# Post-LN layer with a test-time-trained attention scan: three turns moved to TensorE, and the order of VectorE, SyncE and ScalarE work changed

## The reference, cut to what matters

```
k = rotary(x @ Wk.T); v = x @ Wv.T                # per head, 32 features
W = eye(32)                                       # one state per batch and head
for each mini-batch of 16 tokens:
    z = kc @ W
    W = W - kc.T @ ((z - vc) * 2/(16*32))
x1 = layernorm(x + layernorm(z_all, gamma, beta) @ Wo.T)
g = (x1 @ gate_w.T) * gate_s; u = (x1 @ up_w.T) * up_s    # 1408 features, float32
out = layernorm(x1 + (silu(g) * u) @ down_w.T * down_s)
```

## Time and profile before

| | |
|---|---|
| median of three runs | 2067.89 us |
| the profiled execution's own time | 2065.14 us |
| its span | 2062.9 us |
| TensorE busy, matmuls | 1871.4 us (91%) |
| VectorE busy | 1175.4 us (57%) |
| ScalarE busy | 544.1 us (26%) |
| GpSimd busy | 642.3 us (31%) |
| DMA, queue of SyncE | 47.3% of 16 engines' span |

### The profile page before, as it was taken

How to read it: one execution, slowest core, us unless ns; L and a number is a source line. 1 busy time by engine, 2 the same in 40 slices (tenths; PEclk the granted TensorE clock), 3 DMA queues, 4 the chain that set the end, 5 groups by cost and what they waited for, 6 DMA issues and landing times.

```text
span 2062.9 us, 60543 instructions
## 1 busy us (share of the span) xinstructions
PE 1871.4 (91%) x25752; PEld 1488.1 (72%) x25752; DVE 1175.4 (57%) x2618; ACT 544.1 (26%) x1230; POOL 642.3 (31%) x776
## 2 busy tenths in 40 slices
PE   5556999999999999999999999999999999999897
PEld 4335777777777777777777777777777777777676
DVE  4354655665565566556556655655665565566543
ACT  2012222322222222222222222222322222232222
POOL 1012333333333333333332333333333333333233
PEclk9667999999999999999999999999999999999999
DMA  8583455545445554444455444455545445554310
GB/s 253 182 281 97 124 150 147 156 127 148 142 126 150 147 159 132 141 138 137 141 147 158 134 138 139 125 151 148 157 127 145 142 129 148 145 150 122 109 57 22
DMA packets 306800, 292.48 MB, mean 142 GB/s; under 512 B 42977, under 2 KB 255073, under 8 KB 306529
## 3 DMA queue, kind: packets, MB, share of 16 engines
q1 hardware_dynamic: 305248, 288.07, 47.3%
q10 hardware_dynamic: 1280, 0.53, 0.1%
HBM read 155.27 MB, written 141.82 MB: 144 GB/s over the span
## 4 chain that ended last, share of the span: by engine, by line
PE 63%; DMA 15%; DVE 11%; SPq 4%; issue 3%; ACT 3%; ACTq 0%; POOL 0%; DVEq 0%; POOLq 0%
PE gu_acc L755 26%; PE work L736 21%; PE down_acc L767 9%; DMA landed<-zT_scr 8%; DMA zT_scr<-turned 4%; PE scan_acc L725 3%; PE scan_acc L708 3%; SPq L336 2%; DVE turned L896 2%; DVE state L964 2%; DVE x_tok L891 2%; ACT hid L586 2%; DVE hid L969 2%; DMA z_scr<-v_rows 1%; DVE k_sin L946 1%
## 5 line engine op out<-in xcount | busy, mean ns | idle before, releaser
L520 POOL TENSOR_TENSOR hid_lo<-hid,hid_hi 128x256 fp32r<-128x256 f32 x352 | 262.0, 744 | 795.9 <-ACT hid_hi L596 795.8
L755 PE MATMUL gu_acc<-x_hi,gw 128*128 128x256 f32 x1372 | 377.6, 308 | 7.2 <-DVE hid L969 2.0
L586 ACT ACTIVATE hid<-gu_acc,gate_scale 128x256 f32<-128x256 f32 x343 | 162.6, 474 | 769.2 <-PE gu_acc L755 767.8
L755 PE MATMUL gu_acc<-x_hi,uw 128*128 128x256 f32 x1372 | 344.5, 283 | 0.0
L755 PE MATMUL gu_acc<-x_lo,uw 128*128 128x256 f32 x1372 | 343.1, 281 | 0.0
L755 PE MATMUL gu_acc<-x_lo,gw 128*128 128x256 f32 x1372 | 342.6, 281 | 0.0
L964 DVE SCALAR_TENSOR_TENSOR state<-scan_acc,half_step,state 128x256 f32<-128x256 f32 x512 | 223.1, 477 | 199.3 <-PE scan_acc L725 195.5
L969 DVE SCALAR_TENSOR_TENSOR hid<-gu_acc,up_scale,hid 128x256 f32<-128x256 f32 x343 | 165.5, 483 | 290.3 <-ACT hid L586 290.3
L755 PEld LDWEIGHTS gu_acc<-x_hi,gw 128*128 128x128 f32 x1372 | 257.5, 188 | 43.3 <-DVE hid L969 17.0
L767 PE MATMUL down_acc<-dw,hid_hi 128*128 128x512 f32 x704 | 282.3, 401 | 2.2 <-POOL hid_lo L520 2.1
L767 PE MATMUL down_acc<-dw,hid_lo 128*128 128x512 f32 x704 | 278.8, 396 | 0.0
(11 more groups left out here) (88 smaller groups left out, 2133.9 us busy)
## 6 DMA issues: line engine op xcount, KB each, us to landing
x_fm<-xT SPq DMA_DIRECT2D x64, 256.0 KB, 3.4
k_scr<-k_tok SPq DMA_DIRECT2D x32, 512.0 KB, 6.2
kT_scr<-turned SPq DMA_DIRECT2D x128, 128.0 KB, 2.9
kT<-kT_scr SPq DMA_DIRECT2D x32, 512.0 KB, 3.4
k_rows<-k_scr SPq DMA_DIRECT2D x512, 32.0 KB, 2.0
z_scr<-v_rows SPq DMA_DIRECT2D x32, 512.0 KB, 3.1
z_tok<-z_scr SPq DMA_DIRECT2D x512, 32.0 KB, 1.8
x_tok<-x SPq DMA_DIRECT2D x32, 512.0 KB, 3.9
```

Of the source, the lines that this page charges most:

```text
L520: pool.tensor_tensor(hid_lo[m % RING][:], hid[m % 2][:], hid_hi[m % RING][:].bitcast(F32), ALU.subtract).then_inc(hid_lo_ready, 1)
L586: act.activation(hid[m % 2][:], gu_bank(n, m)[:, 0:TOK], ACT.Silu, scale=gate_scale[:, m:m + 1]).then_inc(silu_done, 1)
L755: mm = pe.matmul(gu_bank(n, m)[:, k * TOK:(k + 1) * TOK], lhsT=w[:, c, m * P:(m + 1) * P].bitcast(dt), rhs=part[:, c].bitcast(dt), start=( ...
```

## The change

On TensorE, k of tiles 0, 1 and 2 (tick 0 slot 3, ticks 1 and 2 slot 6), zn of tile 0 (tick 2 slot 4) and x1 of tile 0 (tick 2 slot 10) are turned by transposes into PSUM. ScalarE copies k from PSUM to kT (`copy_kT`). VectorE's turns and the DRAM trips of these five are gone. On VectorE, both halves of `turn_zn` stand together ahead of `scale_hid` in slot 2; `normalize(2)` stands behind the statistics of zn in slot 0; `rotate(t+1, 0)` stands at the end of slot 12. On SyncE, the load of turned zn follows its store directly, the load of x comes behind it, and `out` is stored behind v of batch 0. FFN copies and loads go to ScalarE's queue: 10 copies (gate in 2, up in 4, down in 4) and 11 loads, one per scan slot or so. v rows of tile 1 go to that queue too. The buffer `half_step` is allocated later. The diff, cut to its core:

```
 SyncE, tick(t):
                 if within(sc) and sc >= 1:
                     load_k_half1(sc)
+                if within(sc) and sc >= ROW_TILES:
+                    load_v_half1(sc)
+                if within(t):
+                    store_v(t, 0)
                 if within(y):
                     sp.wait_ge(y_ready, 2 * y + 2)
                     sp.dma_start(out[...], y_tok[:]).then_inc(out_stored, 16)
-                if within(sc) and sc >= 1:
-                    load_v_half1(sc)
-                if t == 2:
-                    load_ffn(0, 0)
-                    load_ffn(0, 1)
-                if within(t):
-                    store_v(t, 0)
-                if within(o) and o != LAST:
+                if within(o) and z_by_dma(o):
                     store_znT(o)
+                    load_znT(o)
                 if within(o):
                     load_x(o)
-                if within(o) and o != LAST:
-                    load_znT(o)
...
-                if within(t) and t >= 1:
+                if within(t) and k_by_dma(t):
                     store_kT(t)
...
-                if within(t + 2):
+                if within(t + 2) and t != 1:
                     load_x_fm(t + 2)
...
+                if t == 1:
+                    load_x_fm(t + 2)

 ScalarE:
+            def load_v_rows(n, half):
+                act.wait_ge(v_stored, 32 * n + 32)
+                if n >= 1:
+                    act.wait_ge(state_added, 4 * NS * (n - 1) + 2 * NS * (half + 1))
+                    act.wait_ge(z_stored, 48 * (n - 1) + (16, 48)[half])
+                for g in range(NG):
...
+            def copy_kT(n, b):
+                act.wait_ge(k_turned, 2 * n + b + 1)
+                if n >= 1:
+                    act.wait_ge(k_cols_ready, 4 * n)
+                act.activation(kT[...], k_turn_bank(n, b)..., ACT.Copy).then_inc(kT_in, 8)
...
+                        copy_ffn(0, 0, 2)
+                    if within(t) and not k_by_dma(t) and s == 6:
+                        copy_kT(t, 0)
+                        copy_kT(t, 1)
+                    if t == 0 and s == 12:
+                        copy_ffn(0, 2, NC)
+                    if t == 1 and s in (0, 2, 4, 6):
+                        copy_ffn(1, s // 2, s // 2 + 1)
+                    if t == 1 and s in (8, 10, 12, 14):
+                        copy_ffn(2, 3 * (s // 2 - 4), min(3 * (s // 2 - 3), NM))
+                    if t == 2 and s in (0, 1, 2, 3):
+                        load_ffn(0, s, s + 1)
+                    if t == 2 and s in (4, 5, 6, 7):
+                        load_ffn(1, s - 4, s - 3)
+                    if t == 2 and s in (8, 9, 10):
+                        load_ffn(2, 4 * (s - 8), min(4 * (s - 7), NM))
+                    if t == 1 and s == 10:
+                        load_v_rows(1, 0)
+                    if t == 2 and s == 2:
+                        load_v_rows(1, 1)

 TensorE:
+            def turn_k(n):
+                if n == 0:
+                    pe.wait_ge(small_in, 16 * SMALL)
+                elif n == 1:
+                    pe.wait_ge(v_ready, 2)
+                else:
+                    pe.wait_ge(zn_low, 2)
+                for b in range(BATCH):
+                    pe.wait_ge(k_ready, 2 * n + b + 1)
+                    turn(k_turn_bank(n, b), k_tok, b, k_turned)
...
+                    if t == 0 and s == 3 or t in (1, 2) and s == 6:
+                        turn_k(t)
+                    if o == 0 and s == 4 or o == LAST and s == 5:
+                        turn_zn(o)
+                    if within(o) and not z_by_dma(o) and s == 10:
+                        turn_x1(o)

 VectorE, tick(t):
-                    if within(yn) and s == 0:
-                        normalize(2, yn, 0, y_tok, y_tok, y_ready)
-                        normalize(2, yn, 1, y_tok, y_tok, y_ready)
-                    if within(o) and o != LAST and s == 2:
+                    if within(o) and z_by_dma(o) and s == 2:
                         turn_zn(o, 0)
+                        turn_zn(o, 1)
...
-                    if within(t + 1) and s == 13:
-                        rotate(t + 1, 0)
...
                         moments_of(0, o)
+                    if within(yn) and s == 0:
+                        normalize(2, yn, 0, y_tok, y_tok, y_ready)
+                        normalize(2, yn, 1, y_tok, y_tok, y_ready)
...
-                    if within(o) and o != LAST and s == 2:
-                        turn_zn(o, 1)
...
+                    if within(t + 1) and s == 12:
+                        rotate(t + 1, 0)
                     for piece in WEIGHED.get((t, s), ()):
```

More of the change, by code:

```diff
@@ L229, in v_bank, with k_by_dma, kT_before, z_by_dma @@
             return (gu_acc, down_acc[1])[b] if n == 0 else work
-        LAST = NT - 1
+        def k_by_dma(n):
+            return n >= EARLY_TICKS
+        def kT_before(n):
+            return max(0, n - EARLY_TICKS)
+        def z_by_dma(n):
+            return n not in (0, LAST)
+        def zT_before(n):
+            return max(0, min(n, LAST) - 1)
+        def k_turn_bank(n, b):
+            return scan_acc[:, b, :] if n == 0 else (gu_acc, down_acc[1])[b][:]
+        def z_turn_bank(n, b):
+            return scan_acc[:, b, :] if n == LAST else (gu_acc, down_acc[1])[b][:]
         def by_token(buf, b):
@@ L238, in gu_bank, with turned_z @@
             return scan_acc[:, 2, :] if m % 2 and (n == LAST or n == LAST - 1 and m >= 3) else gu_acc[:]
[L240 to L248, removed]
+        def turned_z(n, b):
+            if z_by_dma(n):
+                return by_token(landed, b)
+            return z_turn_bank(n, b).rearrange("p (c a t) -> p c a t", c=NC, t=HEAD)
         def token_blocks(fm_buf, b):
@@ L399, in _ @@
             sp.wait_ge(zeroed, ZEROED)
[L401 to L412, removed]
             def tick(t):
@@ L606, in high_zn @@
             def high_zn(n, b):
-                if n == LAST:
+                if not z_by_dma(n):
                     act.wait_ge(zn_turned, 2 * n + b + 1)
                 elif b == 0:
-                    act.wait_ge(znT_in, 16 * (n + 1))
+                    act.wait_ge(znT_in, 16 * zT_before(n + 1))
                 if within(n + 2):
@@ L625, in high_x1 @@
             def high_x1(n, b):
-                if n == LAST:
+                if not z_by_dma(n):
                     act.wait_ge(x1_turned, 2 * n + b + 1)
                 elif b == 0:
-                    act.wait_ge(x1T_in, 16 * (n + 1))
+                    act.wait_ge(x1T_in, 16 * zT_before(n + 1))
                 if n >= 1:
                     act.wait_ge(gu_done, NM * n)
-                act.activation(token_blocks(x1_hi, b), turned_x1(n, b), ACT.Copy).then_inc(x1_hi_ready, 1)
-            def load_first_v():
-                act.wait_ge(v_stored, 32)
-                for half in range(2):
-                    for g in range(NG):
-                        b, hg = g // NC, g % NC
-                        act.dma_start(v_rows[g * MB:(g + 1) * MB, half * NS // 2:(half + 1) * NS // 2, g % 2, :],
-                                      v_scr[b, half * P // 2:(half + 1) * P // 2, hg * P:(hg + 1) * P]
-                                      .rearrange("(i t) c -> t i c", t=MB)).then_inc(rows_in[half], 16)
+                act.activation(token_blocks(x1_hi, b), turned_z(n, b), ACT.Copy).then_inc(x1_hi_ready, 1)
@@ new lines, in load_v_rows @@
+            def load_v_rows(n, half):
[4 more added lines that the diff above has]
+                for g in range(NG):
+                    b, hg = g // NC, g % NC
+                    act.dma_start(v_rows[g * MB:(g + 1) * MB, half * NS // 2:(half + 1) * NS // 2, g % 2, :],
+                                  v_scr[b, half * P // 2:(half + 1) * P // 2, hg * P:(hg + 1) * P]
+                                  .rearrange("(i t) c -> t i c", t=MB)).then_inc(rows_in[half], 16)
@@ L644, in _, with load_ffn @@
+            def load_ffn(i, c0, c1):
+                dst, src = ((gw, gw_scr), (uw, uw_scr), (dw, dw_scr))[i]
+                act.wait_ge(ffn_copied[i], 16 * COPIES[i])
+                act.dma_start(dst[:, c0:c1].bitcast(F32), src[c0 * P:c1 * P].rearrange("(c p) n -> p c n", p=P)
+                             ).then_inc(ffn_in[i], 16)
             act.wait_ge(wk_in, 16 * NC)
@@ L900, in turn_zn @@
                 dve.wait_ge(zn_ready, 2 * n + b + 1)
-                if b == 0 and n >= 1:
-                    dve.wait_ge(x1T_stored, 64 * n)
+                if b == 0 and n >= 2:
+                    dve.wait_ge(x1T_stored, 64 * zT_before(n))
                 turn(z_tok, b, zn_turned)
```

121 lines of the change are left out of this document (55 added, 66 removed).

## The result

The changed kernel takes 1959.34 us, the median of 4 runs (1953.75 to 1960.84). The kernel before takes 2068.91 us (4 runs, 2067.1 to 2076.71). The ratio is 0.9459, with a 95% interval of 0.9427 to 0.949. The profiled execution took 1957.84 us, its span 1956.0.

What follows compares the result with a forecast made beforehand. TensorE was taken as the bound in usual ticks, a chain of waits at the start. From 2065.14 us: -37 rotation, -31 zn, +14 normalize, -22 start gives 1989.1, 1992 with the median's 2.75; predicted 1991, range 1965 to 2028.

Steps and rivals of the forecast that it cites:

- item 3: Start: tile 0's z stores no longer queue behind a weight copy or v rows, so z's statistics come 10.5 us earlier.
- C: Rival: the moved normalize costs nothing and the zn residue is 0, giving 1971 us; chance 0.09.
- rotation: Slot 12: rotating ahead of the state update removes project_v's 1.33 us wait for the rotary product; 37 us in all.
- (a): Slot 2: the second zn turn, ahead of scale_hid, makes both turns end 0.9 us earlier.
- (b): SyncE's queue: turned zn, loaded ahead of x, lands up to 1.7 us sooner.
- 0.5 us for out: SyncE's queue: delay of the zn trip from out being stored just ahead of the store of zn.
- residue of 0.2 us a tick: project_o(0): zn wait expected to remain because single waits reach 3.0 us; 6 us in all.
- (1): Start, tick 0: turning tile 0's k on TensorE and copying it on ScalarE delays the row loads; cost 1.7 us.
- (2): Start, tick 1: turn_k adds 2.1 us behind scan_z, offset by the error step and earlier rotation; together 0.
- (4): Start: TensorE's turns of tile 0's zn replace project_o's 10.46 us wait for the DRAM trip; gain 4.2 us.
- (5): Start: the 6.65 us wait for tile 0's turned x1 and VectorE's two x1 turns go; gain 8 us.
- (6): Start: from VectorE's last weigh piece to TensorE's next work nothing changes; 0.

Runs made afterwards that it cites:

- a2: The kernel before with only rotate(t+1, 0) moved to the end of slot 12: 2032.68 us, ratio 0.9807.
- a4: The kernel after with the load of x issued ahead of the load of turned zn again: 1975.39 us, ratio 0.9533.
- b2: a3 with the second zn turn back behind scale_hid in slot 2: 1957.41 us, ratio 0.9446.
- b1: a3 with out stored ahead of the v rows of the scan's second half, as before: 1946.64 us, ratio 0.9392.
- d3: The kernel before with both zn turns ahead of scale_hid and turned zn loaded ahead of x: 2022.4 us, ratio 0.9762.
- b3: a3 with all four gate loads issued in slot 2 of tick 2 instead of slots 0 to 3: 1950.22 us, ratio 0.9405.
- c2: The kernel before with only the FFN weight copies and loads moved to ScalarE's queue, in pieces: 2067.64 us, ratio 0.9982.
- c4: The kernel after with only tick 2's rotation back in slot 13, behind the state update: 1963.51 us in one execution.
- c3: The kernel after with tile 0's zn and x1 turned by VectorE over DRAM again: 1967.94 us, ratio 0.9497.
- d2: The kernel after with the FFN weights back on SyncE's queue in their old pieces and places: 1964.78 us, ratio 0.9476.
- d1: The kernel before with all edits outside the start (rotation, zn turns, loads, out, normalize, half_step): 1981.33 us, ratio 0.9561.
- b4: The kernel after with 32 unused bytes per partition added where half_step stood before: 1963.01 us, ratio 0.9466.
- a1: The kernel before with only half_step allocated behind rstd: 2068.87 us, ratio 0.9987.
- c1: The kernel after with 64 unused bytes per partition added where half_step stood before: 1958.59 us, ratio 0.9453.
- a3: The kernel after with normalize(2) back in its old place ahead of scale_hid: 1947.19 us, ratio 0.9393.

## Why the prediction was wrong

The direction, the bound and the mechanisms of the tick's terms stood; in the start one reason was wrong (item 3 below). None of the rivals happened; C is nearest in time (1971), but the normalize wasn't free. What failed is the size of five terms, all on one side; together they miss some 30 us, which is the gap between 76 and 107:

| term | forecast | measured | what failed |
|---|---|---|---|
| rotation | -37 | -44 | the stretch is longer than the printed idle |
| zn | -31 | -37 | the residue kept for single long waits |
| normalize(2) | +14 | +8 | 0.48 a tick; it is 0.28 |
| half_step's place | no term | -4 to -8 | not costed |
| start | -22 | -27.5 | items 2, 4 and 6 |

- **Rotation.** "The wait goes" was right. Its value was read from the idle column (1.33 us), which counts from the modelled end of the last matmul. The groups before show it: 1.47 us more from start to start, and 0.09 in the matmuls that refill behind it. a2 alone shows the same 1.55; its medians show 37.5 us.
- **zn.** Both (a) and (b) hold (a4, b2). The 0.5 us for out is nothing (b1). The residue of 0.2 us a tick is 0.02 (0.5 us in 2 waits). With the wait went the stretches at the lower clock behind it (6.8 us before, none in d3): 0.12 us a tick in project_o(0).
- **normalize(2).** I let both of its instructions count in full but for the cover of 0.69 us. The state update started 0.91 us behind the normalize's start, not 1.1.
- **The tick as a check.** The prediction's mark "ticks about 57.4 us apart" came true at 57.34, and that was luck. It was worked out from a single tick of about 59.4; the mean spacing before was 60.2, so the terms as sized would have given 58.3. The sum (54 us in 28 ticks) and the mark contradicted each other: (60.2 - 57.4) x 28 is 78. Comparing them would have shown 24 us missing.
- **Start.** Item by item, forecast and measured: (1) +1.7, +1.5. (2) 0, -4.2: tile 1's first scan_z comes at 78.27 where it was 80.97, though k is turned in between. The rotation gave 1.3 as foreseen. The rest is the granted clock, 1.00 from 50 to 62 us where it had been 0.93, 0.65 and 0.78 in three stretches of 4 us, and project_v behind the rotation, before and after:
```profile
74.46 2.92 PE L736 MATMUL work<-wv,fm 128*128 128x512 f32 x6 [2.46 <-DVE k_sin L946]
```
```profile
73.02 1.66 PE L755 MATMUL work<-wv,fm 128*128 128x512 f32 x6 [1.12 <-DVE k_sin L982]
```
Before, TensorE had waited 2.46 us and then ran at half speed; after, 1.12 and at full. What of it is owed to turn_k's work wasn't tried. (3) -10.5, the 1.7 included; measured -9.3. z of the last step was saved at 76.1, 4.4 us ahead of my 80.5, but its store left only at 81.31: the loads ahead of it on SyncE's queue waited for the store before. It then took 6.31 us beside the gate loads (b3). The last store before, and the two stores after:
```profile
95.08 1.78 DMA z_scr<-v_rows
```
```profile
74.33 4.02 DMA z_scr<-v_rows
...
81.31 6.31 DMA z_scr<-v_rows
```
The first of the two (384 KB) fell from the 8.53 us of the earlier trace rows, behind a copy of 1280 KB (not 1.5 MB), to 4.02; the last rose from 1.78 to 6.31. Together they took 10.3 us before and 10.3 after, so of the two reasons that the prediction gave for item 3 the shorter store gained nothing. The whole 9.3 us is that the first store left at 74.33 instead of 83.81: the other reason, v rows, and the next x and rot, which the prediction didn't count, together 6.3 us of issues, no longer stand between the k rows and it, nor does the copy (0.57), and the k rows begin 2.4 us earlier. What each of them is worth wasn't tried by itself; c2, which leaves all but the copy there, lets the store go at 81.24. (4) -4.2, -7.0: z's turns and project_v behind the earlier rotation. (5) -8, -7.6. (6) 0, -3.6: GpSimd's rows weren't read, and the row that says "issue" hid a wait on it (c4). Parts of (4) and (5) together are c3's 10 us; the queue is 5 to 8 (c2, d2). Of the five misses this one is the least sure: the end of the start moves by some 6 us between executions, and by the medians of d1 the start's own edits are worth 22 to 24, which is what was forecast for them.

The range was too narrow for terms that shared one way of being read. The ends of the unknown costs were kept for each edit, but no end was kept for the basis: printed idle, one profiled execution that was among the quickest of before, and an allocation taken as free.

## What to carry over

Value a wait by the distance from start to start of the work around it, averaged over all its places, and not by its idle column; then check the sum against the spacing of whole ticks. A wait on a trip of fixed length (turn, store, load) can take up what other edits gain in the same tick. No run here shows it clear of the spread: by the medians a2 and d3 give 37.5 and 50.6 us alone, less 12 for normalize and with 4 to 8 for half_step 80 to 84, and all together (d1) 91.6, a difference about as large as the intervals. Before a profile is held against another, look at how far the executions of one kernel lie apart: a wait that differs in c2 from before by 9 us in the sum, in ticks that nobody edited, explains nothing by itself. Where VectorE has its idle time before a wait, work moved out of it costs: 0.28 us a tick here, 12 us by the medians, and taking that one edit back gives the best kernel of the study with b1, 1947.19 us.

## What the runs showed of the hardware

- The place of a matmul's moving operand in memory counts at the level of a per cent: a gate/up unit of 16 matmuls takes 2.014 and 2.015 us (before, b4) with x1_hi and x1_lo 32 bytes further than in after, a1 and c1 by the worked-out addresses, modulo 64, and 1.989 to 1.998 there.
- GpSimd's all-reduce over partitions began 5.6 to 6.0 us behind the end of the instruction before it in the five kernels where its operand was there sooner (5.61 in before, 5.67 in c2, 5.65 in c4, 5.60 in d3, 5.99 in a1).
- Eight fp32 transposes of 128x128 by TensorE took 1.04 us at 21.23 us (tile 0's k), at a granted clock of 1.00, and 1.97 us from 98.77 us (z), where it was 0.50.
- A 128 KB store on SyncE's queue took 1.78 and 2.81 us with no load of the weights issued just ahead (before, b3), 3.87 us when two of 704 KB had gone out on ScalarE's queue 4.66 us ahead (a3), and 6.31 when they had 1.86 us ahead (after).
- b2 and a3 have ticks of 57.17 and 57.10 us in their profiled executions and medians 10 us apart: one profile doesn't rank kernels that stand this near to a wait.
